# A causal convolution fed by Toeplitz loads: its inputs loaded by group, in rows of 4 KB, behind the four Toeplitz loads

## The reference, cut to what matters

```python
def conv(u, length, ...):                       # u: 32 sequences x 64 channels x 1024 steps
    mask = arange(L) < length[:, None]
    u_m = u * mask[:, None, :]
    kernel = _get_kernel(log_dt, C, log_A_real, A_imag, L)      # one row of 1024 taps per channel
    y = irfft(rfft(u_m, n=2*L) * rfft(kernel, n=2*L))[..., :L]   # causal convolution along time
    return (y + u_m * D[:, None]) * mask[:, None, :]

def ffn(hid, gate_w, u, g, d):                  # 16 experts of 112 hidden columns, the best 2 per row
    w = top-2 softmax weights of hid @ gate_w.T
    h = silu(hid @ g.T) * (hid @ u.T)
    return sum over experts of w * (h @ d.T)

out = x + ffn(conv(x, lengths, ...), ...)
```

## Time and profile before

| | |
|---|---|
| median of 3 runs | 492.87 us |
| the profiled execution's own time | 494.46 us |
| its span, first to last instruction | 492.7 us |
| TensorE busy | 437.4 us (89%) |
| VectorE, ScalarE, GpSimd busy | 196.3, 108.9, 168.8 us |
| mean granted TensorE clock, as a share of full speed | 0.972 |
| moved by DMA | 115.99 MB, mean 235 GB/s |
| first and last convolution product | 33.6 us, 211.1 us |

### The profile page before, as it was taken

How to read it: one execution, slowest core, us unless ns; L and a number is a source line. 1 busy time by engine, 2 the same in 40 slices (tenths; PEclk the granted TensorE clock), 3 DMA queues, 4 the chain that set the end, 5 groups by cost and what they waited for, 6 DMA issues and landing times.

```text
span 492.7 us, 9187 instructions
## 1 busy us (share of the span) xinstructions
PE 437.4 (89%) x2880; PEld 381.5 (77%) x2880; DVE 196.3 (40%) x525; ACT 108.9 (22%) x257; POOL 168.8 (34%) x213
## 2 busy tenths in 40 slices
PE   0359999999899998779689999999999999999991
PEld 0359999989899998768578878888877888887770
DVE  6924434444434353577213333333333333333330
ACT  3880000000100000080012222222222222222220
POOL 4543332222223100001663334446344344543322
PEclk9999999999999999979779999999999999999997
DMA  8976898999899988993984897996997796775550
GB/s 283 342 211 213 258 299 262 293 292 298 261 315 292 283 263 255 331 338 143 348 306 110 252 292 152 297 277 182 286 266 208 196 279 151 158 163 85 87 75 16
DMA packets 46491, 115.99 MB, mean 235 GB/s; under 512 B 10098, under 2 KB 25714, under 8 KB 46322
## 3 DMA queue, kind: packets, MB, share of 16 engines
q1 hardware_dynamic: 25138, 73.49, 46.6%
q0 software_dynamic: 12096, 33.58, 29.5%
q10 hardware_dynamic: 9216, 8.39, 5.6%
HBM read 93.63 MB, written 40.66 MB: 273 GB/s over the span
## 4 chain that ended last, share of the span: by engine, by line
PE 72%; DMA 13%; DVE 5%; ACT 3%; SPq 2%; issue 2%; POOL 1%; POOLq 0%; DVEq 0%; ACTq 0%
PE conv_ps L1200 25%; PE conv_ps L1057 20%; PE conv_ps L1219 14%; PE turn_ps L1209 7%; DMA k_rows<-k_sb 6%; DMA arena<-k_rows 4%; DMA arena<-y_rows,from_row 2%; PE k_bank L1115 2%; PE turn_ps L1068 1%; DVE tmp L666 1%; ACT arena L528 1%; ACT arena L580 1%; SPq L336 1%; PE conv_ps L1226 1%; SPq L335 1%
## 5 line engine op out<-in xcount | busy, mean ns | idle before, releaser
L1057 PE MATMUL conv_ps<-arena 128*128 128x256 f32 (+7 forms) x1024 | 155.6, 308 | 10.0 <-DMA arena<-k_rows 9.9
L1057 PEld LDWEIGHTS conv_ps<-arena 128*128 128x128 f32 x1024 | 147.6, 191 | 17.7 <-issue 7.5
L1200 PE MATMUL conv_ps<-arena,ys_t 128*128 x640 | 130.8, 358 | 1.9 <-DVE ys_t L1004 1.9
L1200 PEld LDWEIGHTS conv_ps<-arena,ys_t 128*128 128x128 f32 x640 | 120.4, 194 | 14.2 <-issue 13.7
L479 POOL DMA_INDIRECT out<-arena,from_row x40 | 62.9, 1571 | 125.7 <-DMA out<-arena,from_row 81.5
L1219 PE MATMUL conv_ps<-arena,hid_t 112*128 x160 | 75.5, 594 | 1.0 <-DVE hid_t L1019 1.0
L771 DVE TENSOR_TENSOR arena<-conv_ps,mask_t 128x256 f32<-128x256 f32 x64 | 27.1, 424 | 92.0 <-PE conv_ps L1057 91.0
L1012 DVE TENSOR_TENSOR hid<-silu,conv_ps 128x112 f32<-128x112 f32 x40 | 10.9, 271 | 105.0 <-ACT silu L620 100.1
L1024 DVE TENSOR_SCALAR arena<-conv_ps,slot_weight 128x512 f32<-128x512 f32 x40 | 30.0, 751 | 42.6 <-PE conv_ps L1219 41.6
L1219 PEld LDWEIGHTS conv_ps<-arena,hid_t 112*128 112x128 f32 x160 | 27.2, 190 | 21.0 <-issue 21.0
L409 POOL TENSOR_TENSOR am<-wave,cs_re 128x128 f32<-128x128 f32 x16 | 6.5, 404 | 104.5 <-ACT wave L544 101.6
(11 more groups left out here) (175 smaller groups left out, 355.9 us busy)
## 6 DMA issues: line engine op xcount, KB each, us to landing
arena<-k_rows SPq DMA_DIRECT2D x64, 512.0 KB, 6.5
arena<-gu_t SPq DMA_DIRECT2D x16, 896.0 KB
y_rows<-y_blk ACTq DMA_DIRECT2D x64, 128.0 KB, 2.9
arena<-x_time SPq DMA_DIRECT2D x56, 128.0 KB, 5.5
arena<-d_t SPq DMA_DIRECT2D x16, 448.0 KB
arena<-x_time SPq DMA_DIRECT2D x2, 512.0 KB, 5.9
out<-arena,from_row POOLq DMA_INDIRECT x44
out<-ys SPq DMA_DIRECT2D x1, 512.0 KB, 7.4
```

What stands on the lines that cost most here:

```text
L1057: last = nc.tensor.matmul(conv_ps[:, h, d * B:C * B], toep[:, p, h, d * P:(d + 1) * P], u_t[:, p, h, 0:(C - d) * B], start=(d == 0), stop= ...
L1200: last = nc.tensor.matmul(gu_ps, ys_t[:, t % 2, c, :], flat[:, bass.ds(bufs[t] * WE + c * GU, GU)], start=(c == 0), stop=(c == C - 1))
```

## The change

The per-channel input load disappears from SP's loop. After the four Toeplitz loads of a group of 2 or more, SP issues one load of the inputs of all four channels (128 rows of 4 KB, 512 KB), which counts on `u_in[p]`. On TensorE `convolve` waits for `u_in[p]` once, ahead of the group's first channel, and `toep_in[p][h]` rises by 16 per group instead of 32. Nothing else changes; groups 0 and 1 are as before.

```diff
@@ SP, for g in range(G), for h in range(HG)
                     if g >= 2:
                         sp.wait_ge(conv_done, (g - 2) * HG + h + 1)
-                        sp.dma_start(u_t[:, p, h, :], x_time[:, g * HG + h, :]).then_inc(toep_in[p][h], 16)
                     sp.dma_start(toep[:, p, h, :], bass.AP(k_rows, (g * HG + h) * KROW, [[1, P], [1, L]])
                                  ).then_inc(toep_in[p][h], 16)
+                if g >= 2:
+                    sp.dma_start(u_t[:, p, :, :], x_time[:, g * HG:(g + 1) * HG, :]).then_inc(u_in[p], 16)
@@ TensorE
             def convolve(g, p, i, second=False, counting=False):
+                pe.wait_ge(u_in[p], 16 * (i + 1))
                 for h in range(HG):
...
-                    pe.wait_ge(toep_in[p][h], 32 * i + 16)
+                    pe.wait_ge(toep_in[p][h], 16 * (i + 1))
                     convolve_channel(g, h, p, False)
```

## The result

| | before | after |
|---|---|---|
| median beside each other on one chip | 491.8 us (489.02 to 493.02, 4 runs) | 504.78 us (502.82 to 506.32, 4 runs) |
| ratio | | 1.027, 95% interval 1.0208 to 1.0331 |
| profiled span | 492.7 us | 504.5 us |
| start of group 15's products | 200.83 us | 212.40 us |
| SP's loop, mean of groups 3 to 14 | 11.27 us | 11.64 us |

The changed kernel is slower by 13.0 us. The prediction was 499.5, between 490.2 and 508: the time lies inside, but the slowdown is nearly twice the 6.6 us forecast.

What follows compares the result with a forecast made beforehand. The convolution stage was taken as bound by DMA transfers plus the round trip ending each SP loop. Group 15 starting at 59.2 + 13 x 11.4 = 207.4, 6.6 us later, gave 492.87 + 6.6 = 499.5 us, range 490.2 to 508.

Steps and rivals of the forecast that it cites:

- The mechanism: Convolution: inputs land last, one loop after SP's start; TensorE starts later, row stores fall among loads; 6.6 us slower.
- no change that can be told: Rival: SP's loop between 10.7 and 11.08 us just pays back TensorE's later start; 493 us, chance 0.16.
- much slower: Rival: row stores and loads collide in every SP loop, lengthening it to 12.2 us; 509.9 us, chance 0.18.
- The sum: SP begins group 3 at 59.2; thirteen loops of 11.4 put group 15 at 207.4, 6.6 us later.
- twelve loops: SP's loops from group 3 to group 15, forecast at 11.4 us each against 11.27 before.
- The sum of the parts: SP's loop: Toeplitz loads and store 8.53 to 9.06 us, inputs 1.4, row stores 1.4; 11.3 to 11.9 in all.
- Rows of 4 KB: Input load in 4 KB instead of 1 KB rows: a difference of 0.1 us a group.
- The estimate of up to 6 us: Saving per group from three DMAs fewer at about 2 us fixed cost; the prediction held the trace contradicted it.
- Three issues fewer: SP's loop: the taps' store is issued some 1.4 us earlier but still lands behind the loads; gain zero.
- `k_added`: SP's wait before storing taps: ready 2.6 us into the loop, about when wanted, waiting at most a microsecond.
- nothing here feeds on itself: TensorE's later start does not hold up SP; a one-time shift of about the loop less 5.3 us.
- The faster rival: SP's loop drops to TensorE's 10.6 us and TensorE stops waiting; 489.1 us, chance 0.14.

Runs made afterwards that it cites:

- run 1: The changed kernel with the group's one input load ahead of the four Toeplitz loads instead of behind them: 489.14 us, 0.9944 of the kernel before.
- run 2: The kernel before with its four per-channel input loads issued behind the four Toeplitz loads: 506.3 us, ratio 1.0283.
- run 9: The changed kernel with the group's input load between the second and third Toeplitz load: 497.13 us, 1.0108 of the kernel before.
- run 3: The changed kernel with row stores cut to one channel of four and the gather reading rows of x: 491.54 us, 0.9959 of the kernel before.
- run 4: The kernel before with row stores cut to one channel of four and the gather reading rows of x: 490.62 us, ratio 0.9964.
- run 11: The changed kernel with the store of the next group's taps issued ahead of the inputs' load: 489.73 us, 0.9948 of the kernel before.
- run 12: The changed kernel with the group load in front and the next group's taps stored ahead of the fourth Toeplitz load: 485.98 us, 0.9877 of the kernel before.
- run 10: The kernel before with all four per-channel input loads ahead of the four Toeplitz loads: 506.86 us, ratio 1.0306.
- run 6: The changed kernel with the taps of groups 4 to 15 stored by ACT, three groups ahead: 508.48 us, 1.0334 of the kernel before.
- run 5: The kernel before with the taps of groups 4 to 15 stored by ACT, three groups ahead: 487.53 us, ratio 0.9906.

## Why the prediction was right, and where its sum was off

**The mechanism held.** Slower, because the inputs land last, one loop after SP began the group; because of that TensorE starts later, and ACT issues its row stores among the loads. Runs 1, 2 and 9 show that the place costs and not the load; runs 3 and 4 that the longer loops come with the row stores, for without three quarters of them the medians show no cost of the change; runs 11 and 12 that both need a store that stands last. That the time fell inside the range is owed in part to its width: the range also held "no change that can be told" and the lower part of "much slower".

**The sum was 5 us short.** It had group 15 start 6.6 us later; it starts 11.57 later, and the span is 11.8 longer. The twelve loops account for more than half of the gap: 1.6 us in the sum (11.4 for 11.27), 4.5 measured. Term by term, from the two traces:

| term | predicted | measured | difference |
|---|---|---|---|
| SP begins group 3 | 59.2 | 60.60 | +1.4 |
| twelve loops | 11.4 each | 11.64 each | +2.9 |
| landing of group 15's inputs after SP's start | 11.4 | 10.8 | -0.6 |
| TensorE's start after that landing | 0 | 1.3 | +1.3 |

The first isn't the change's: up to group 2 the two kernels do the same, and the profiled executions differ by 1.7 us there (48.32 and 46.66). The loop was mis-sized by a choice. The sum of the parts gave 11.3 to 11.9, and I took a value near the lower end because I hoped that the slow start of a loop would take in some row stores free. The measured 11.64 is the middle; in the loop shown above the row stores didn't move at its start at all but mostly in its last 3 us. The last term was not in the sum: I had put the cost of TensorE's waits at nothing beyond their length, while the clock was at half speed after three of them, and the third made group 14's products outlast the landing of group 15's inputs.

**Rows of 4 KB.** My term was 0.1 us a group, from 53 against 50 us of engine time per MB. Where the change puts the load, behind the four, its form is worth 0.23 us per loop (11.87 to 11.64, one trace each), twice my figure; in front it is 1.19 us (run 10). The mean times per MB that I compared, of two different queues, showed neither. SP's own queue comes closer: its share fell from 46.6% of 492.7 us to 44.5% of 504.5 for the same 73.49 MB, by which I estimate 0.4 us for each of 14 groups. The rule of the Trainium skill that I had set beside it ("DMA: Bandwidth & Descriptors", "Rules for kernel authors": coalesce many small transfers) is borne out in front of the loop. The estimate of up to 6 us from the same page's fixed cost is not: 3 fewer DMAs gave 1.19 us at most. The Trainium skill gives that figure of about 2 us ("Anatomy of one DMA" on the same page) for DMAs issued by GpSimd, and these are SP's.

**Three issues fewer**: nothing gained that the runs show, as said. The store went out 1.4 us earlier in the loop shown, 1.2 in the mean of twelve (3.0 us into a loop for 4.2), and took longer to land: 8.7 us in the median for 7.0.

**`k_added`.** I had it wanted and ready at about the same time, with a wait of at most a microsecond. SP waited for it 5.6 us in 4 pieces, the longest 2.3, so the place was right and single waits were larger. So "nothing here feeds on itself" was too strong: this closes a ring over three groups, which run 6 made visible.

**The faster rival** had the loop drop to TensorE's pace. It needed what runs 11 and 12 did by hand, a store that isn't last (in the kernel before, run 5 got there with the store on ACT's queue).

## What to carry to other kernels

Ask of a wait on a transfer not only which transfer it names but where that stands in its queue: moved from the front of the queue to the back, the same 512 KB went from a gain of 0.6% to a loss of 2.7%. When a consumer starts later, follow what it sends out, since those transfers move as well and may leave the only gap that they had. And where a small store has to land before the next loads may be issued, put it ahead of the last big load: here that took the time from 2.7% above the kernel before to 0.5% below it.

## What the runs showed of the hardware that I had not expected

- A store of 16 KB on ACT's own queue took 8.1 us to land in the median, beside SP's loads and behind ACT's row stores (run 6); behind the loads in SP's queue it had taken 7.0 before and 8.7 in the changed kernel. The Trainium skill says in "DMA: Bandwidth & Descriptors", section "Issuing engines are not separate DMA queues", that DMAs issued by different engines run on the same 16 DMA engines and interleave; these figures are its price here, though how much of them is ACT's own row stores isn't shown.
- With four loads of 128 KB ahead of 2 MB, the first 5 us of a loop moved 212 GB/s in the mean of twelve loops, where one load of 512 KB had 255 (runs 10 and 1); the loops were 12.10 and 10.91 us. The cause wasn't found.
- Waits of TensorE of 4.6, 1.8 and 2.2 us (at 60, 107 and 200 us) were each followed by 3.4 us at the lower clock level, 1.2 GHz for 2.4. In the kernel before a wait of 2.5 us ahead of group 15 was not the earlier trace rows: its products took 2.49 us.
